# One wide product for the four window sums of a message tile, its diagonal blocks kept and folded

## The chip, the core and the metric

The kernel runs on one NeuronCore of a Trainium2 chip. The metric is the device time in microseconds (us) of one execution. The core has a matrix engine (PE, with its weight loads shown apart as PEld), a vector engine (DVE), a scalar engine (ACT), GpSimd (POOL), which here issues the gathers, and SyncE (SP), which issues the other DMAs. Each engine works through its own instructions in order, and they signal each other by semaphores.

## The reference

The reference is two graph layers on 12500 nodes of 96 features, with 412500 edges sorted by their target node. What matters here is the first layer's message step:

```python
edge_feat = _mlp(edge_attr, W_edge, b_edge, g_edge, beta_edge)
message = jnp.concatenate([x[row], x[col], edge_feat], axis=1)
message = _mlp(message, W_msg, b_msg, g_msg, beta_msg)      # relu(h @ W + b), then a norm over all edges
agg = jax.ops.segment_sum(message, col, num_segments=n)     # sum of the messages of each target node
```

The norm's mean and variance are taken over all edges, so the kernel sums, for each target node, the raw relu outputs and a column of ones, and beside it the squares of all messages; the norm is applied afterwards to the sums.

## The kernel before, in words

Edges are cut into 806 super tiles of 512 edges, four tiles (SUP = 4) of 128 edges each. As edges are sorted by target, the targets of one super tile lie in a window of W = 32 consecutive nodes that begins at `base`. "Tile" below means such a super tile. The program runs through four stretches: a node stage, a first pass over the edges for the statistics of the edge features (in which every sixth tile's gathered rows are also fetched and spilled to memory), the message stage (about 935 to 4340 us), and then the second layer.

The message stage is the one that is changed. It is written out in full, 806 times, on each engine. `msgs.run(engine, step, lag)` calls `step` for k = 0, 1, 2, ... and a step treats tile k in some functions and an earlier one, `msgs.earlier(i, k, n)`, in others. There is no planner: the order of each engine is the order of the calls in its step, and `Signal` objects say what waits for what. For one tile:

- ACT copies the 4 index columns (`copy_indices`, L923), and POOL then gathers 4 x 128 rows of `a_tab` with four indirect DMAs (`gather`, L932), into one of four buffers. The tile that follows in every sixth place is not gathered: SP loads what was spilled (`load_spilled`). A buffer is free when DVE has added its rows (m_pre of tile k-4).
- SP loads the edge features, the target numbers and the window's rows of `b_tab`.
- PE forms the edge product (`edge_product`, L983, bf16, 512 columns); ACT takes its relu into `lhs` (`edge_relu`, L990). DVE writes the transposed one-hots into the lowest 32 rows of `lhs` (`onehot_T`, L998), the window's rows into `rhs` (`window_rows`, L975) and the one-hots `oh` (`onehot`, L1005: 128 edges by 4 x 32).
- PE forms four message products in fp32 (`message_product`, L1017), DVE adds the gathered rows (`add_gathered`, L1030), ACT takes the relu into `msg` (`message_relu`, L1038; 96 columns, and a 97th of ones) and the square (`square`, L1045), which DVE sums up (`accumulate`, L1052).
- PE sums the messages by target (`sum_edges`, L1061): four fp32 products, weights `msg` of 128 x 97, moving `oh` of 128 x 32, that accumulate in one 97 x 32 block of PSUM. DVE adds this block to 32 columns of the node sums `sT` (`add_window`, L1071).

The order of one step k: PE edge_product(k), message_product(k-1), sum_edges(k-2). ACT copy_indices(k), edge_relu(k-2), message_relu(k-3), square(k-3). DVE onehot_T(k), window_rows(k), onehot(k), add_gathered(k-1), accumulate(k-2), add_window(k-2). POOL only gathers, tile after tile. An fp32 product shows in the profile as two records on PE and two on PEld.

Of the kernel before, what the change touches and what calls it, by code (L numbers as in the profile page):

```python
# [17 lines left out]
ALU = mybir.AluOpType  # L18
ACT = mybir.ActivationFunctionType
AX = mybir.AxisListType.X  # L20
# [3 lines left out]
C = 96  # L24
# [4 lines left out]
SUP = 4  # L29
ES = TILE * SUP  # L30
W = P - C
# [64 lines left out]
def gnn_kernel(nc, d, a, out):  # L96
# [4 lines left out]
    with ctx:  # L101
# [7 lines left out]
        def sem(name):  # L109
            stage_sems.append(nc.alloc_semaphore(name))  # L110
            return stage_sems[-1]

        def signal(name, ahead):
            return Signal(sem(name), ahead)
# [33 lines left out]
        ident = sb("ident", [P, P])  # L148
# [39 lines left out]
        msg = sb("msg", [P, 2, SUP, C + 1])  # L188
        sq = sb("sq", [P, 2, SUP, C])
        acc = sb("acc", [P, SUP, C])  # L190
        oh = sb("oh", [P, 4, SUP, W])
        psum = ctx.enter_context(nc.psum_tensor("psum", [P, 8 * 512], FP32))
        bank = [psum[:, i * 512:(i + 1) * 512] for i in range(8)]


        x_flat = x_all[:, :, :].rearrange("p t c -> p (t c)")
# [682 lines left out]
        MT = 2 * SPILL  # L879
        msgs = Turns(SV, MT)  # L880
# [5 lines left out]
        r_mm = signal("r_mm", 4)  # L886
        r_ok = signal("r_ok", 2)
        ohT_ok = signal("ohT_ok", 4)
        oh_ok = signal("oh_ok", 0)
        m_mm = signal("m_mm", 2)  # L890
# [2 lines left out]
        m_sq = signal("m_sq", 2)  # L893
        m_acc = signal("m_acc", 2)
        s_mm = signal("s_mm", 4)
        s_add = signal("s_add", 2)
        def was_spilled(k):
            return k % SPILL == SPILL - 1

# [14 lines left out]
            return bank[2 + k % 2][:, 0:SUP * C].rearrange("p (t c) -> p t c", t=SUP)  # L914

        def ps_s(k):
            return bank[4 + k % 2][0:C + 1, 0:W]

        def copy_indices(act, i, k):
            if msgs.absent(i, k) or was_spilled(k):  # L920
# [131 lines left out]
            dve.tensor_tensor(acc[:, :, :], acc[:, :, :], sq[:, k % 2, :, :], ALU.add).then_inc(m_acc.sem, 1)  # L1052

        def sum_edges(pe, i, k):
            if msgs.absent(i, k):
                return
            pe.wait_ge(m_ok.sem, m_ok.at(MT * i + k))
            pe.wait_ge(oh_ok.sem, oh_ok.at(MT * i + k))
            pe.wait_ge(s_add.sem, s_add.at(MT * i + k - 2))
            for t in range(SUP):  # L1060
                ins = pe.matmul(ps_s(k), msg[:, k % 2, t, :], oh[:, k % 4, t, :], start=(t == 0), stop=(t == SUP - 1))  # L1061
            ins.then_inc(s_mm.sem, 1)

        def add_window(dve, i, k):
            if msgs.absent(i, k):
                return
            base = dve.value_load(base_i[:, bass.ds(MT * i + k, 1)], min_val=0, max_val=N - 1)
            dve.wait_ge(s_mm.sem, s_mm.at(MT * i + k))
            dve.wait_ge(s_add.sem, s_add.at(MT * i + k - 1))
            cols = sT[0:C + 1, bass.ds(base, W)]  # L1070
            dve.tensor_tensor(cols, cols, ps_s(k), ALU.add).then_inc(s_add.sem, 1)  # L1071

        y = gbuf[:, :, :, :].rearrange("p k t c -> p (k t c)")
# [162 lines left out]
        with nc.If(windowed):  # L1242
            with nc.Block() as block:
                @block.gpsimd
                def _(g):
                    def step(i, k):
                        gather(g, i, k)
                    msgs.run(g, step, 0)

                @block.sync  # L1250
                def _(sp):
                    def step(i, k):
                        load_pair(sp, i, k)
                        load_window(sp, i, k)
                        load_spilled(sp, i, k)
                    msgs.run(sp, step, 0)

                @block.tensor
                def _(pe):
                    for x in (r_mm, m_mm, s_mm):  # L1260
                        x.start(pe)
                    def step(i, k):
                        edge_product(pe, i, k)
                        message_product(pe, *msgs.earlier(i, k, 1))
                        sum_edges(pe, *msgs.earlier(i, k, 2))
                    msgs.run(pe, step, 2)

                @block.scalar
                def _(act):
                    for x in (r_ok, m_ok, m_sq):  # L1270
                        x.start(act)
                    def step(i, k):
                        copy_indices(act, i, k)
                        edge_relu(act, *msgs.earlier(i, k, 2))
                        message_relu(act, *msgs.earlier(i, k, 3))
                        square(act, *msgs.earlier(i, k, 3))
                    msgs.run(act, step, 3)

                @block.vector
                def _(dve):  # L1280
                    dve.memset(sT[:, 0:NP], 0.0).then_inc(m0, 1)
                    dve.memset(acc[:, :, :], 0.0).then_inc(m0, 1)
                    dve.wait_ge(m0, 2)
                    for x in (ohT_ok, w_ok, m_pre, m_acc, s_add):
                        x.start(dve)
                    def step(i, k):
                        onehot_T(dve, i, k)
                        window_rows(dve, i, k)
                        onehot(dve, i, k)
                        add_gathered(dve, *msgs.earlier(i, k, 1))  # L1290
                        accumulate(dve, *msgs.earlier(i, k, 2))
                        add_window(dve, *msgs.earlier(i, k, 2))
                    msgs.run(dve, step, 2)
        with nc.Else():
            general_pass("_m", True)

# [700 lines left out]
```

## Time and profile before

| what | value |
|---|---|
| median of the runs | 6518.5 us (6517.94, 6518.5, 6523.41) |
| the profiled execution | 6520.64 us |
| its span, first to last instruction | 6518.9 us |
| PE busy over the span | 5654.6 us (87%) |
| PEld busy | 4382.9 us (67%) |
| DVE busy | 4173.9 us (64%) |
| ACT busy | 3822.2 us (59%) |
| POOL busy | 3237.0 us (50%) |
| mean granted clock of PE | 0.650 |

A row of a group has the line, the engine and the operation, then the written and read tiles with their shapes (partitions x elements, type) and the count, and behind the bar the busy time in us, the mean of one in ns, and the engine's idle time just before these instructions with what ended it. "issue" is idle time in which the engine waited for nothing that the profile shows. In a timeline row the first number is the start in us from the span's start, the second the length. In a windows row the five busy times are those of PE, PEld, DVE, ACT and POOL, in this order, unless the row is of one engine alone. A busy PE is not PE at its peak: matmuls are pipelined and their ends are modelled, so consecutive records overlap.

### The profile page before, as it was taken

To read this page: it belongs to the slowest core of one execution; us is meant where nothing else is said; L and a number is where in the kernel's file an instruction comes from. 1 tells how busy PE (TensorE), PEld (TensorE's weight loads), DVE (VectorE), ACT (ScalarE), POOL (GpSimd) and SP (SyncE) were. 2 spreads that over 40 slices of the span, in tenths; PEclk is the share of its full clock that TensorE was granted. 3 is DMA by queue.
4 is the path that set the end of the run, shared out by engine and by line. 5 is a ranking of instruction groups with operands and counts; after the bars stand their busy time and mean duration, and the time that the engine had idled before them with its cause. 6 is when DMAs were issued, how large, how long until landed. Compare 5 with 4: busy or idle time off the path is not lost. (4 is left out here: it accounts for less than half of the span.)

```text
span 6518.9 us, 128731 instructions
## 1 busy us (share of the span) xinstructions
PE 5654.6 (87%) x38038; PEld 4382.9 (67%) x38038; DVE 4173.9 (64%) x13072; ACT 3822.2 (59%) x7170; POOL 3237.0 (50%) x3406
## 2 busy tenths in 40 slices
PE   6755559999999999999999999977799999999998
PEld 5311127777777777777777777765477777777777
DVE  5577764545454544445454444553799999999996
ACT  3566644434444444444444444433699999999996
POOL 3577757777777777777777777753000000000000
PEclk8555555555555555555555555555799999999998
DMA  4444433333333333333333333321000000000001
GB/s 155 137 123 124 124 83 74 74 76 75 76 75 76 74 76 74 74 76 75 75 75 76 74 75 75 74 79 30 18 2 2 2 2 2 2 2 2 2 2 62
DMA packets 297570, 400.07 MB, mean 61 GB/s; under 512 B 146679, under 2 KB 203015, under 8 KB 296247
## 3 DMA queue, kind: packets, MB, share of 16 engines
q1 hardware_dynamic: 193543, 233.00, 12.1%
q0 software_dynamic: 103344, 158.83, 11.5%
q8 instruction: 323, 5.29, 0.3%
q14 instruction: 360, 2.95, 0.1%
HBM read 333.74 MB, written 57.67 MB: 60 GB/s over the span
## 5 line engine op out<-in xcount | busy, mean ns | idle before, releaser
L932 POOL DMA_INDIRECT gbuf<-a_tab,idxb x2688 | 2580.4, 960 | 859.0 <-issue 812.3
L1718 ACT ACTIVATE nf<-psum 128x600 bf16<-128x600 f32 x3234 | 1824.2, 819 | 4.8 <-PE psum L1709 4.8
L1017 PEld LDWEIGHTS psum<-rhs,lhs 128*128 128x128 f32 x6448 | 1434.3, 327 | 365.8 <-issue 365.8
L1017 PE MATMUL psum<-rhs,lhs 128*128 128x96 f32 x6448 | 1628.7, 434 | 13.5 <-DVE rhs L975 13.5
L1038 ACT ACTIVATE msg<-pre 128x384 f32<-128x384 f32 x806 | 421.8, 523 | 1991.2 <-DVE pre L1030 1988.7
L1030 DVE TENSOR_TENSOR pre<-psum,gbuf 128x384 f32<-128x384 f32 x806 | 448.2, 556 | 1613.6 <-issue 1130.0
L1709 PE MATMUL psum<-x_all 128*128 128x300 bf16 x6468 | 1358.8, 291 | 121.6 <-DVE x_all L1702 44.6
L1061 PE MATMUL psum<-oh,msg 128*97 128x32 f32 x6448 | 1171.1, 344 | 282.4 <-ACT msg L1038 276.7
L1061 PEld LDWEIGHTS psum<-oh,msg 128*97 128x97 f32 x6448 | 1134.0, 282 | 364.1 <-ACT msg L1038 358.7
L1701 DVE TENSOR_SCALAR x_all<-x_all,dstrel 128x600 bf16<-128x600 f16 x3234 | 1193.8, 369 | 87.4 <-PE psum L1709 63.0
L1731 PE MATMUL psum<-x_all,nf 128*128 128x96 bf16 x15400 | 1074.4, 205 | 1.0 <-ACT nf L1718 1.0
L1731 PEld LDWEIGHTS psum<-x_all,nf 128*128 128x128 bf16 x15400 | 937.7, 97 | 165.9 <-issue 1.8
L1702 DVE TENSOR_SCALAR x_all<-x_all,src_i 128x128 bf16<-128x128 bf16 x3234 | 788.2, 244 | 0.0
L1709 PEld LDWEIGHTS psum<-x_all 128*128 128x128 bf16 x6468 | 421.5, 96 | 360.8 <-DVE x_all L1702 241.8
L793 PE MATMUL psum<-x_all,w 36*96 36x512 bf16 x806 | 394.4, 638 | 280.7 <-DMA x_all<-attr_parts 278.1
L836 DVE BATCH_NORM_STATS2 sT<-x_all 96x6 f32<-96x512 f32 x806 | 493.1, 676 | 181.0 <-ACT x_all L813 180.5
L744 POOL DMA_INDIRECT gbuf<-a_tab,idxb x536 | 506.0, 944 | 179.3 <-issue 150.6
L813 ACT ACTIVATE x_all<-psum,par 96x1024 f32<-96x1024 f32 x403 | 425.5, 1105 | 231.7 <-PE psum L793 229.1
L990 ACT ACTIVATE lhs<-psum,par 96x512 f32<-96x512 f32 x806 | 539.2, 669 | 3.9
L983 PE MATMUL psum<-x_all,w 36*96 36x512 bf16 x806 | 530.9, 659 | 4.5 <-DMA x_all<-attr_parts 4.4
L793 PEld LDWEIGHTS psum<-x_all,w 36*96 36x96 bf16 x806 | 118.0, 180 | 556.5 <-DMA x_all<-attr_parts 490.3
L1052 DVE TENSOR_TENSOR acc<-acc,sq 128x384 f32<-128x384 f32 x806 | 441.9, 548 | 0.6 <-ACT sq L1045 0.6
(198 smaller groups left out, 3340.3 us busy)
## 6 DMA issues: line engine op xcount, KB each, us to landing
gbuf<-a_tab,idxb POOLq DMA_INDIRECT x3224
x_all<-dst_row SPq DMA_DIRECT2D x403, 128.0 KB
x_all<-attr_parts SPq DMA_DIRECT2D x807, 36.0 KB
x_all<-attr_parts SPq DMA_DIRECT2D x1209, 24.0 KB
spilled<-gbuf SPq DMA_DIRECT2D x134, 192.0 KB, 1.9
gbuf<-spilled SPq DMA_DIRECT2D x134, 192.0 KB
x_all<-b_tab SPq DMA_DIRECT2D x806, 12.0 KB
attr_parts<-sT SPq DMA_DIRECT2D x72, 136.0 KB, 1.9
```

Source lines behind the costliest of these rows:

```text
L744: g.indirect_dma_start(gbuf[:, j, t, :], None, a_tab[:, :], bass.IndirectOffsetOnAxis(ap=idxb[:, j, t:t + 1], axis=0)).then_inc(x_land[j], 16)
L793: pe.matmul(bank[k % 6][0:C, :], w36[:, :], ek[:, q % NB, k % HG, :], start=True, stop=True).then_inc(e_mm.sem, 1)
L932: g.indirect_dma_start(gbuf[:, k % 4, t, :], None, a_tab[:, :], bass.IndirectOffsetOnAxis(ap=idxb[:, k % 4, t:t + 1], axis=0)).then_inc(g_ ...
L983: pe.matmul(ps_r(k), w36[:, :], rk[:, (k // HP) % 2, k % HP, :], start=True, stop=True).then_inc(r_mm.sem, 1)
L990: act.activation(lhs[0:C, k % 2, :], ps_r(k), ACT.Relu, bias=par[:, B_EDGE:B_EDGE + 1]).then_inc(r_ok.sem, 1)
L1017: ins = pe.matmul(ps_m(k)[:, t, :], lhs[:, k % 2, t * TILE:(t + 1) * TILE], rhs[:, k % 2, :], start=True, stop=True)
L1061: ins = pe.matmul(ps_s(k), msg[:, k % 2, t, :], oh[:, k % 4, t, :], start=(t == 0), stop=(t == SUP - 1))
L1701: dve.tensor_scalar(o_key[:, n % 3, :], iota_k, key_f[:, n:n + 1], None, ALU.is_equal)
L1702: dve.tensor_scalar(o_lo[:, n % 3, :], iota_l, lo_f[:, n:n + 1], None, ALU.is_equal).then_inc(e_oh, 1)
L1709: ins = pe.matmul(ps_a(n)[:, b, :], o_lo[:, n % 3, :], o_key[:, n % 3, b * HB:(b + 1) * HB], start=True, stop=True)
L1718: act.activation(adj[:, g % 2, :, j * SLOT:(j + 1) * SLOT].rearrange("p (b h) s -> p b h s", b=2), ps_a(n).rearrange("p b (h s) -> p b h s ...
L1731: ins = pe.matmul(ps_b(g), adj[:, g % 2, h, :], t3[:, h, :], start=(h == 0), stop=(h == HI - 1))
```

## The change

The four window sums of a tile become one fp32 product. Its weights are all four one-hots side by side (128 edges x 128 columns), its moving operand all four message tiles side by side (128 edges x 4 x 97 = 388 columns). Of the 128 x 388 result only the four diagonal blocks of 32 x 97 are wanted (one-hots of tile t with messages of tile t). ACT copies these four from PSUM into a buffer `diag` of 128 partitions x 97 (`keep_blocks`). A second product (`fold_blocks`), weights `diag` (128 x 97), moving `sel` (128 x 32, four identity matrices of 32 stacked), adds the four blocks and gives the same 97 x 32 block as before, in another bank. DVE adds that to `sT`.

`sel` is made once from the identity by a reduction on DVE, and PE waits for it at the start of the stage. The new order of a step k: PE edge_product(k), message_product(k-1), sum_edges(k-2), fold_blocks(k-4). ACT as before, then keep_blocks(k-4). DVE as before, but add_window(k-5) in place of add_window(k-2). `d_ok`, `f_mm` and the two buffers of `diag` and of the folded block tie these together.

```diff
--- before.py
+++ after.py
@@ -893,7 +893,13 @@
         m_sq = signal("m_sq", 2)
         m_acc = signal("m_acc", 2)
         s_mm = signal("s_mm", 4)
+        d_ok = signal("d_ok", 2)
+        f_mm = signal("f_mm", 2)
         s_add = signal("s_add", 2)
+        sel_ok = sem("sel_ok")
+        X0 = 6 * ES + 2 * C
+        sel = x_flat[:, X0:X0 + W]
+        diag = x_flat[:, X0 + W:X0 + W + 2 * (C + 1)].rearrange("p (b c) -> p b c", b=2)
         def was_spilled(k):
             return k % SPILL == SPILL - 1
 
@@ -914,7 +920,10 @@
             return bank[2 + k % 2][:, 0:SUP * C].rearrange("p (t c) -> p t c", t=SUP)
 
         def ps_s(k):
-            return bank[4 + k % 2][0:C + 1, 0:W]
+            return bank[4 + k % 2][:, 0:SUP * (C + 1)]
+
+        def ps_f(k):
+            return bank[6 + k % 2][0:C + 1, 0:W]
 
         def copy_indices(act, i, k):
             if msgs.absent(i, k) or was_spilled(k):
@@ -1052,28 +1061,42 @@
             dve.tensor_tensor(acc[:, :, :], acc[:, :, :], sq[:, k % 2, :, :], ALU.add).then_inc(m_acc.sem, 1)
 
         def sum_edges(pe, i, k):
+
             if msgs.absent(i, k):
                 return
             pe.wait_ge(m_ok.sem, m_ok.at(MT * i + k))
             pe.wait_ge(oh_ok.sem, oh_ok.at(MT * i + k))
+            pe.wait_ge(d_ok.sem, d_ok.at(MT * i + k - 2))
+            pe.matmul(ps_s(k), oh[:, k % 4, :, :].rearrange("p t w -> p (t w)"),
+                      msg[:, k % 2, :, :].rearrange("p t c -> p (t c)"), start=True, stop=True).then_inc(s_mm.sem, 1)
+
+        def keep_blocks(act, i, k):
+
+            if msgs.absent(i, k):
+                return
+            act.wait_ge(s_mm.sem, s_mm.at(MT * i + k))
+            act.wait_ge(f_mm.sem, f_mm.at(MT * i + k - 2))
+            for t in range(SUP):
+                ins = act.activation(diag[t * W:(t + 1) * W, k % 2, :],
+                                     ps_s(k)[t * W:(t + 1) * W, t * (C + 1):(t + 1) * (C + 1)], ACT.Copy)
+            ins.then_inc(d_ok.sem, 1)
+
+        def fold_blocks(pe, i, k):
+
+            if msgs.absent(i, k):
+                return
+            pe.wait_ge(d_ok.sem, d_ok.at(MT * i + k))
             pe.wait_ge(s_add.sem, s_add.at(MT * i + k - 2))
-            for t in range(SUP):
-                ins = pe.matmul(ps_s(k), msg[:, k % 2, t, :], oh[:, k % 4, t, :], start=(t == 0), stop=(t == SUP - 1))
-            ins.then_inc(s_mm.sem, 1)
+            pe.matmul(ps_f(k), diag[:, k % 2, :], sel, start=True, stop=True).then_inc(f_mm.sem, 1)
 
         def add_window(dve, i, k):
             if msgs.absent(i, k):
                 return
             base = dve.value_load(base_i[:, bass.ds(MT * i + k, 1)], min_val=0, max_val=N - 1)
-            dve.wait_ge(s_mm.sem, s_mm.at(MT * i + k))
+            dve.wait_ge(f_mm.sem, f_mm.at(MT * i + k))
             dve.wait_ge(s_add.sem, s_add.at(MT * i + k - 1))
             cols = sT[0:C + 1, bass.ds(base, W)]
-            dve.tensor_tensor(cols, cols, ps_s(k), ALU.add).then_inc(s_add.sem, 1)
-
-
-
-
-
+            dve.tensor_tensor(cols, cols, ps_f(k), ALU.add).then_inc(s_add.sem, 1)
 
 
         y = gbuf[:, :, :, :].rearrange("p k t c -> p (k t c)")
@@ -1257,29 +1280,34 @@
 
                 @block.tensor
                 def _(pe):
-                    for x in (r_mm, m_mm, s_mm):
+                    for x in (r_mm, m_mm, s_mm, f_mm):
                         x.start(pe)
+                    pe.wait_ge(sel_ok, 1)
+
                     def step(i, k):
                         edge_product(pe, i, k)
                         message_product(pe, *msgs.earlier(i, k, 1))
                         sum_edges(pe, *msgs.earlier(i, k, 2))
-                    msgs.run(pe, step, 2)
+                        fold_blocks(pe, *msgs.earlier(i, k, 4))
+                    msgs.run(pe, step, 4)
 
                 @block.scalar
                 def _(act):
-                    for x in (r_ok, m_ok, m_sq):
+                    for x in (r_ok, m_ok, m_sq, d_ok):
                         x.start(act)
                     def step(i, k):
                         copy_indices(act, i, k)
                         edge_relu(act, *msgs.earlier(i, k, 2))
                         message_relu(act, *msgs.earlier(i, k, 3))
                         square(act, *msgs.earlier(i, k, 3))
-                    msgs.run(act, step, 3)
+                        keep_blocks(act, *msgs.earlier(i, k, 4))
+                    msgs.run(act, step, 4)
 
                 @block.vector
                 def _(dve):
                     dve.memset(sT[:, 0:NP], 0.0).then_inc(m0, 1)
                     dve.memset(acc[:, :, :], 0.0).then_inc(m0, 1)
+                    dve.tensor_reduce(sel, ident[:, :].rearrange("p (t w) -> p w t", w=W), AX, ALU.add).then_inc(sel_ok, 1)
                     dve.wait_ge(m0, 2)
                     for x in (ohT_ok, w_ok, m_pre, m_acc, s_add):
                         x.start(dve)
@@ -1289,8 +1317,8 @@
                         onehot(dve, i, k)
                         add_gathered(dve, *msgs.earlier(i, k, 1))
                         accumulate(dve, *msgs.earlier(i, k, 2))
-                        add_window(dve, *msgs.earlier(i, k, 2))
-                    msgs.run(dve, step, 2)
+                        add_window(dve, *msgs.earlier(i, k, 5))
+                    msgs.run(dve, step, 5)
         with nc.Else():
             general_pass("_m", True)
```

## Rows read from the trace of the kernel before

**Rows 1.** Windows view: span, busy us (count) by engine, clock, DMA share, GB/s

```profile
935.00:4343.00 3408.00, 3119.88 (x13700) 2635.78 (x13701) 1689.52 (x4836) 1383.05 (x3087) 2580.38 (x2688) 0.50 0.31 75
```

**Rows 2.** Waits view of 945 to 4330 us: us in total, times, longest

```profile
DVE pre L1030 <- issue: 1130.0, 424, 5.3
POOL gbuf L932 <- issue: 809.5, 2656, 0.3
DVE pre L1030 <- PE psum L1017: 474.9, 245, 5.2
```

**Rows 3.** Page, costliest groups: busy us, mean ns, idle before and its releaser

```profile
L932 POOL DMA_INDIRECT gbuf<-a_tab,idxb x2688 | 2580.4, 960 | 859.0 <-issue 812.3
...
L1061 PE MATMUL psum<-oh,msg 128*97 128x32 f32 x6448 | 1171.1, 344 | 282.4 <-ACT msg L1038 276.7
```

**Rows 4.** Timeline of POOL: start us, length us, then what

```profile
2621.27 1.17 POOL L932 DMA_INDIRECT gbuf<-a_tab,idxb  x1 [0.30 <-issue]
...
2629.03 0.94 POOL L932 DMA_INDIRECT gbuf<-a_tab,idxb  x1 [0.30 <-issue]
...
2646.68 1.17 POOL L932 DMA_INDIRECT gbuf<-a_tab,idxb  x1 [0.30 <-issue]
```

**Rows 5.** Timeline of PE, a stretch without waits

```profile
2608.19 2.02 PE L1017 MATMUL psum<-rhs,lhs 128*128 128x96 f32 x8
2610.01 1.41 PE L1061 MATMUL psum<-oh,msg 128*97 128x32 f32 x8
2611.34 0.66 PE L983 MATMUL psum<-x_all,w 36*96 36x512 bf16 x1
2611.93 2.02 PE L1017 MATMUL psum<-rhs,lhs 128*128 128x96 f32 x8
```

**Rows 6.** Groups by form, whole span, nearest shapes on PE, ACT and DVE

```profile
L1493 PE MATMUL psum<-gbuf,wc 97*33 97x512 f32 x26 | 24.9, 1061 | 0.0
...
L344 PE MATMUL psum<-dstrel,ones 1*128 1x462 f32 x14 | 11.1, 984 | 7.5 <-DVE flag_f L381 7.5
...
L1483 ACT ACTIVATE gbuf<-psum 97x512 f32<-97x512 f32 x13 | 7.7, 596 | 26.4 <-PE psum L1474 26.4
...
L1616 ACT ACTIVATE wc<-psum 96x32 f32<-96x32 f32 x1 | 0.2, 193 | 2.9 <-PE psum L1600 2.9
...
L1739 DVE TENSOR_REDUCE pre<-psum 128x32 f32<-128x96 f32 x154 | 38.5, 250 | 4.6 <-PE psum L1731 4.6
```

**Rows 7.** Page, costliest groups, weight loads

```profile
L1017 PEld LDWEIGHTS psum<-rhs,lhs 128*128 128x128 f32 x6448 | 1434.3, 327 | 365.8 <-issue 365.8
...
L1061 PEld LDWEIGHTS psum<-oh,msg 128*97 128x97 f32 x6448 | 1134.0, 282 | 364.1 <-ACT msg L1038 358.7
```

**Rows 8.** Windows view of L932 alone, gathers up to 2629 us: busy us (count)

```profile
935.00:2629.00 1694.00, 1285.39 (x1340) 0.50 0.31 75
```

**Rows 9.** Timeline of ACT

```profile
2606.14 0.52 ACT L1045 ACTIVATE sq<-msg 128x384 f32<-128x384 f32 x1
...
2606.67 0.67 ACT L990 ACTIVATE lhs<-psum,par 96x512 f32<-96x512 f32 x1
...
2622.18 0.19 ACT L923 ACTIVATE idxb<-src_i 128x4 int32<-128x4 int32 x1
```

**Rows 10.** Timeline of DVE

```profile
2611.55 0.19 DVE L1071 TENSOR_TENSOR sT<-sT,psum 97x32 f32 x1 [0.27 <-PE psum L1061]
2611.77 0.71 DVE L998 TENSOR_SCALAR lhs<-x_all,winid 32x512 f32<-32x512 int32 x1
...
2621.75 0.49 DVE L998 TENSOR_SCALAR lhs<-x_all,winid 32x512 f32<-32x512 int32 x1
```

**Rows 11.** Timeline, the stage's first gather

```profile
935.19 0.94 POOL L932 DMA_INDIRECT gbuf<-a_tab,idxb  x1 [40.05 <-ACT idxb L923]
```

**Rows 12.** Timeline, the last tile's sum on PE and addition on DVE

```profile
4338.39 1.51 PE L1061 MATMUL psum<-oh,msg 128*97 128x32 f32 x8 [2.81 <-ACT msg L1038]
...
4340.04 0.19 DVE L1071 TENSOR_TENSOR sT<-sT,psum 97x32 f32 x1 [0.56 <-PE psum L1061]
```

## Prediction

> **What bounds the kernel now.** The change touches only the message stage, so I first read the windows view from the stage's first gather to its end [rows 1]: 3408 us of the span of 6518.9, at a granted clock of 0.50, which is the 1.2 GHz level. PE is busy for 3120 us of it (92%), POOL for 2580 (76%), ACT for 1383. By those shares PE looks like the bound. The waits view says otherwise [rows 2]: POOL, 2656 times out of its 2688 gathers in the stage, waited only 0.3 us and for nothing that the profile shows ("issue"), 809.5 us in all. The grouped row gives 960 ns of work for one gather [rows 3]. A gather then comes every 0.960 + 0.305 = 1.265 us. Five tiles in six gather four times (the sixth was spilled and comes back on SP's queue): 20 x 1.265 / 6 = 4.22 us a tile, and 806 tiles make 3399 us. That is the stage. The timeline of POOL shows the cycle: two long gathers at the same place of the pattern, 2621.27 and 2646.68, are 25.41 us apart, with 20 gathers between them [rows 4]. So POOL's issuing of gathers is the bound and never pauses.
>
> PE has room. In a stretch where it waits for nobody, one message product starts at 2608.19 and the next at 2611.93: 3.74 us a tile, in the parts 1.82 (message product), 1.33 (L1061, 2610.01 to 2611.34) and 0.59 (edge product) [rows 5]. That leaves 4.22 - 3.74 = 0.48 us a tile. DVE waits 475 us for PE's L1017 in its L1030, and 1130 us for gathered rows [rows 2]: one tile in six is late by PE, and it is the tile behind the spilled one, whose rows are not urgent.
>
> **The change, part by part.**
> (a) Removed from PE: four products of 97 weight columns and 32 moving columns. L1061 is busy 1171.1 us over 806 tiles, 1.45 us a tile, 0.363 for one product [rows 3].
> (b) Added to PE: one fp32 product with 128 weight columns and 4 x 97 = 388 moving ones. The trace has no such shape. Seven products of 128 by 462 columns (two records each) take 11.1 us, 1.586 each, 3.43 ns a column (L344) [rows 6]: 388 columns are 1.33 us. The isolated ones of 512 columns take 24.9 / 13 = 1.92 us, 3.74 ns a column with their tail (L1493) [rows 6]: 1.45. I take 1.33, since the neighbours keep PE fed.
> (c) Added to PE: the fold, 97 weight columns and 32 moving ones, which is the shape of L1061: 0.363 us.
> Sum on PE: 1.33 + 0.36 - 1.45 = +0.24 us, 3.98 a tile against 4.22. From below: if the wide product hides a weight load of the fold, half of the 0.363, it is +0.06. From above: the slower rate, and one weight load unhidden before each new product (0.327 and 0.282 [rows 7]): 1.45 + 0.36 + 0.33 + 0.28 - 1.45 = 0.97, which would be 4.71; even with one of the two exposed it is 4.38 to 4.43. The nearest row for (b) is the back-to-back one, which has two loads of 128 columns within its 1.586, so I hold to +0.24.
> The Trainium skill, "TensorE: Matmul & The Clock Gate", Part 3 (The mechanism), speaks against that: a weight load overlaps a running matmul only when it goes to another group of rows, and here every one uses all 128 rows. Rows 5 and 7 disagree: eight loads of mean 0.282 add to 2.26 us, and the eight pairs of L1061 pass in 1.41. By that rule both loads of each new product would stand in the open, and the sum would be that of the rival "serial loads" below.
> (d) Added to ACT: four copies PSUM to SBUF of 32 partitions by 97. Two rows enclose them, 96x32 at 193 ns and 97x512 at 596 ns [rows 6]: 0.84 ns a column, so 0.248 each, 0.99 a tile (bounds 0.77 and 2.38). ACT goes from 1383 / 806 = 1.72 to 2.71 us a tile, at worst 4.10, below 4.22. They are queued ahead of the index copy (for which POOL waits), the edge relu (for which PE waits) and the message relu. Their own wait, for the wide product of a tile, is over before ACT gets there: that product is issued two steps of PE earlier, and ACT does a relu and a square (0.52 each) first.
>  - Index copy: the one at 2622.18 belongs to the tile behind the spilled one; its first gather is the one at 2629.03 (1340 gathers lie before it, which is 335 tiles of four [rows 8]). It is 6.7 us early [rows 4, 9]; 1 us off that costs nothing.
>  - Edge relu: in the busiest step the square begins at 2606.14 and the edge relu at 2606.67 [rows 9]. With 1 us between them it ends at 2608.4, when PE wants it at 2608.19 + 0.24 [rows 5]. So one tile in six is later by up to 0.3 us more. It frees the gather buffer of a tile whose gathers start at 2629.03 - 4 x 1.265 = 2624: nobody waits.
> (e) DVE's add_window goes three tiles later, with a wait that is long over. It loses the wait for PE of 0.27 at 2611.55 [rows 10]. The work is the same 806 additions. The one-hot buffer is still four deep and freed by the same signal as before. PE's new waits (for the diagonal copies of two tiles before, for the window sums of two before) end, by the order of the steps, ahead of the message relu that it waits for anyway.
> (f) Ends. At the start DVE reduces 128x128 to 128x32 once; 128x32 from 128x96 takes 0.25 us [rows 6], and the semaphores that let ACT copy the first indices stand behind it: POOL's first gather, at 935.19 after an idle time ended by ACT [rows 11], comes 0.3 us later. At the end the last tile's chain was sum at 4338.39, addition at 4340.04: 1.65 us [rows 12]. Now wide product 1.33 + 0.17 tail, copies 0.99, fold 0.36 + 0.17, handshakes 0.1: 3.1 to 3.3. Plus 1.6.
> Sum of the whole: +1.6 + 0.3 = +1.9 us, call it +2. The profiled execution took 6520.6 us (span 6518.9), the runs shown 6518.5 by their median; so 6522.6 against that execution, and 6520.5 for the median. Where did (a) to (c) go? Into PE's idle time.
>
> **What could still move POOL.** A gather takes 0.94 us in most rows and 0.960 by the mean: 0.020 x 2688 = 54 us are lost in the long ones. They meet L998 on DVE: the gather of 1.17 us began at 2621.27 and L998 at 2621.75, 0.48 into it [rows 4, 10]; at 2611.77 it was L998 itself that took 0.71. Both hold the same resource. L998 follows add_window directly, so (e) shifts it for the one tile in six that waited: 0.27 us earlier by the lost wait, about 0.3 later by (b) to (d). If that one now meets a gather as the one at 2621.27 did, 134 x 0.23 = +31 us; if it met one and now misses, it gives back a share of the 54. Nearest to nought, since the two shifts cancel; I take 0.
>
> **The rivals.**
>  - PE becomes the bound (the other side). It decides once (b) and (c) cost over 1.45 + 0.48 = 1.93 us a tile. With 1.45 + 0.363 and one load of 0.327 in the open they cost 2.14: step 3.74 + 0.69 = 4.43, (4.43 - 4.22) x 806 = +169 us, 6690. For it: PE is already busy 92%, and no row has a 388-column product between narrow ones. Against it: rows 5 and 6 show loads hidden. Chance 0.07.
>  - Serial loads, the same mechanism at its full price: 1.33 + 2 x 0.327 + 0.363 = 2.35 us, step 4.64, +0.42 x 806 = +338 us, 6859. This is the Trainium skill's rule of Part 3 above. Chance 0.03.
>  - L998 meets more gathers: 6551. Chance 0.12.
>  - L998 meets fewer: a third of the 54 us returned, 6502. Chance 0.13.
>  - The wide product, with many more columns a tile, lifts the granted clock from 0.50: PE's step would halve, POOL would still issue every 1.265 us, and only the end would shorten by about 1.5 us: 6519. Chance 0.05.
>  - The forecast: 6520.5, its own range 6508 to 6532. Chance 0.60.
> What a measurement of this kernel can tell from no change is about 0.2%, 13 us. Faster by more: 0.13 (L998 fewer). Slower by more: 0.12 + 0.07 + 0.03 = 0.22. Within: 0.65. The range for 8 in 10 runs from 6500 (all but the best of the fewer-meetings case) to 6560 (over the more-meetings case), and leaves out PE as the bound.
>
> **What the changed profile would show.** PE's step in a stretch without waits 3.9 to 4.1 us; the wide product 1.3 to 1.5 and the fold near 0.36; four ACT copies of about 0.25; POOL's idle time still 0.30 before each gather and its mean near 960 ns; L1071 without a wait for PE; a stage of 3410 us. The prediction is wrong if POOL's idle time is ended by DVE's L1030 or ACT's index copy (PE or ACT had become late), or if the mean gather moves by over 5 ns (13 us).

## The result, and the profile after

The changed kernel takes 6537.2 us (median of 18 runs, 6531.2 to 6542.2) against 6522.3 for the kernel before (18 runs, 6517.9 to 6526.0) beside it. The ratio is 1.0022, with a 95% interval of 1.0015 to 1.0029: about 15 us slower, where +2 was forecast, and a little over the 0.2% (13 us) that the prediction took for no change. It lies inside the predicted range (6500 to 6560), 17 us above the predicted 6520.5 and outside the likeliest case's own range of 6508 to 6532. The profiled execution has a span of 6535.7 us against 6518.9, 16.8 more.

The page's groups of the changed kernel (line, engine, operation, tiles, count | busy us, mean ns | idle before):

```profile
L941 POOL DMA_INDIRECT gbuf<-a_tab,idxb x2688 | 2595.4, 966 | 859.1 <-issue 774.5
...
L1026 PE MATMUL psum<-rhs,lhs 128*128 128x96 f32 x6448 | 1403.5, 387 | 129.0 <-ACT lhs L999 125.5
...
L1070 PE MATMUL psum<-msg,oh 128*128 128x388 f32 x1612 | 1146.5, 809 | 313.9 <-DVE sT L1099 278.0
...
L1080 ACT ACTIVATE x_all<-psum 32x97 f32<-32x97 f32 x3224 | 775.1, 240 | 28.8 <-issue 0.2
```

Against [rows 3], the 2688 gathers are busy 2595.4 us where they were 2580.4, a mean of 966 ns for 960. Their idle time is what it was, 859.1 for 859.0. So 15.0 of the 16.8 us are gathers that took longer, and none is POOL waiting more. The rest stands at the two ends. At the start, with the reduction that makes `sel`:

```profile
934.15 0.24 DVE L1310 TENSOR_REDUCE x_all<-ident 128x32 f32<-128x128 f32 x1
...
935.54 0.94 POOL L941 DMA_INDIRECT gbuf<-a_tab,idxb  x1 [40.42 <-ACT idxb L932]
```

The first gather comes at 935.54, before at 935.19 [rows 11]: +0.35. At the end:

```profile
4348.69 0.95 POOL L941 DMA_INDIRECT gbuf<-a_tab,idxb  x1 [0.30 <-issue]
...
4353.44 0.92 PE L1070 MATMUL psum<-msg,oh 128*128 128x388 f32 x2 [3.62 <-DVE sT L1099]
...
4355.61 0.19 DVE L1099 TENSOR_TENSOR sT<-sT,psum 97x32 f32 x1 [0.64 <-DVE sT L1099]
...
4356.44 0.19 DVE L1099 TENSOR_TENSOR sT<-sT,psum 97x32 f32 x1 [0.64 <-DVE sT L1099]
4357.26 0.19 DVE L1099 TENSOR_TENSOR sT<-sT,psum 97x32 f32 x1 [0.63 <-DVE sT L1099]
```

The last gather ends at 4349.64 and the last window sum begins at 4357.26, 7.62 us later. Before, the last gather ended at 4334.57 and the last window sum began at 4340.04 [rows 12], 5.47 us: +2.15. Sum: 15.0 + 0.35 + 2.15 = 17.5, less 0.3 us of idle time inside the stage and 0.4 behind it.

PE and ACT in the stage. Windows of the whole stage, of a stretch of 18 us and of one of 6 us (us, then busy and count of PE, PEld, DVE, ACT and POOL, granted clock, DMA share, GB/s):

```profile
935.00:4343.00 3408.00, 2967.14 (x10443) 2078.49 (x10442) 1664.56 (x4819) 2199.61 (x6286) 2590.28 (x2683) 0.62 0.32 75
2603.00:2621.00 18.00, 17.48 (x55) 12.30 (x55) 10.42 (x30) 12.79 (x38) 13.73 (x15) 0.50 0.30 71
2624.00:2630.00 6.00, 3.85 (x25) 2.82 (x24) 2.51 (x9) 3.04 (x9) 4.48 (x6) 0.98 0.41 109
```

The granted clock was 0.50 over the stage before [rows 1] and is 0.62 now: it rises to 1.00 and falls back, as the timeline of PE shows, where the same message product takes 2.02 us at 2603.22 and 1.13 at 2624.48.

```profile
2603.22 2.02 PE L1026 MATMUL psum<-rhs,lhs 128*128 128x96 f32 x8
2605.03 1.55 PE L1070 MATMUL psum<-msg,oh 128*128 128x388 f32 x2
2606.38 0.42 PE L1090 MATMUL psum<-x_all 128*97 128x32 f32 x2
2606.73 0.66 PE L992 MATMUL psum<-x_all,w 36*96 36x512 bf16 x1
2607.32 2.02 PE L1026 MATMUL psum<-rhs,lhs 128*128 128x96 f32 x8
...
2611.55 2.02 PE L1026 MATMUL psum<-rhs,lhs 128*128 128x96 f32 x8
...
2624.48 1.13 PE L1026 MATMUL psum<-rhs,lhs 128*128 128x96 f32 x8
...
2626.68 1.13 PE L1026 MATMUL psum<-rhs,lhs 128*128 128x96 f32 x8
```

At the lower level a step is 2607.32 - 2603.22 = 4.10 us (wide product 1.35, fold 0.35), and the next one, 2611.55 - 2607.32, is 4.23; at the higher level a step is 2.20. The three-quarters of the stage at 1.2 GHz did not make PE the bound, and the quarter at 2.4 GHz did not make the kernel faster.

ACT, the step of a tile:

```profile
2604.42 0.52 ACT L1054 ACTIVATE sq<-msg 128x384 f32<-128x384 f32 x1
2604.85 0.99 ACT L1080 ACTIVATE x_all<-psum 32x97 f32<-32x97 f32 x4
...
2606.09 0.68 ACT L999 ACTIVATE lhs<-psum,par 96x512 f32<-96x512 f32 x1
```

The square began at 2604.42 and the edge relu at 2606.09, 1.67 us apart, against 0.53 before [rows 9].

The waits of the stage (us in total, times, longest):

```profile
DVE pre L1039 <- issue: 878.5, 310, 5.0
DVE pre L1039 <- PE psum L1026: 787.7, 356, 5.0
POOL gbuf L941 <- issue: 768.1, 2521, 0.3
...
PEld psum L1026 <- ACT lhs L999: 279.3, 394, 1.3
...
POOL gbuf L941 <- DVE pre L1039: 22.5, 74, 0.3
POOL gbuf L941 <- ACT idxb L932: 21.6, 71, 0.3
...
DVE sT L1099 <- PE psum L1090: 0.3, 1, 0.3
```

DVE's wait for PE before L1039 rose from 475 [rows 2] to 788 us, while its wait there under the name "issue" fell from 1130 to 878.5. PE now waits for ACT's edge relu (L999), 394 times in 806 tiles, so not only for the one tile in six behind a spilled one. DVE's window sum hardly waits for PE any more (once); before, it did so 130 times:

```profile
DVE sT L1071 <- PE psum L1061: 35.8, 130, 0.6
```

POOL's waits for DVE and ACT have a longest of 0.3 us, the same 0.3 that stands before every gather: another name on the same gap.

Which gathers are long? POOL, then DVE:

```profile
2603.87 1.24 POOL L941 DMA_INDIRECT gbuf<-a_tab,idxb  x1 [0.30 <-issue]
...
2607.92 0.94 POOL L941 DMA_INDIRECT gbuf<-a_tab,idxb  x1 [0.30 <-issue]
...
2619.20 1.18 POOL L941 DMA_INDIRECT gbuf<-a_tab,idxb  x1 [0.30 <-DVE pre L1039]
```

```profile
2603.75 0.55 DVE L1061 TENSOR_TENSOR acc<-acc,sq 128x384 f32<-128x384 f32 x1
...
2604.43 0.48 DVE L1007 TENSOR_SCALAR lhs<-x_all,winid 32x512 f32<-32x512 int32 x1
...
2608.46 0.56 DVE L1061 TENSOR_TENSOR acc<-acc,sq 128x384 f32<-128x384 f32 x1
...
2619.01 0.55 DVE L1061 TENSOR_TENSOR acc<-acc,sq 128x384 f32<-128x384 f32 x1
...
2619.70 0.48 DVE L1007 TENSOR_SCALAR lhs<-x_all,winid 32x512 f32<-32x512 int32 x1
```

The prediction blamed DVE's transposed one-hots (now L1007), and they do begin 0.56 us into the gather of 2603.87 and 0.50 into that of 2619.20. But the kernel before has the same start without the loss. Its L998 begins 0.48 us into the gather of 2621.27, which takes 1.17 us [rows 4, 10], and also 0.48 us into that of 2611.29, which takes 0.94:

```profile
2611.29 0.94 POOL L932 DMA_INDIRECT gbuf<-a_tab,idxb  x1 [0.30 <-issue]
```

```profile
2610.73 0.55 DVE L1052 TENSOR_TENSOR acc<-acc,sq 128x384 f32<-128x384 f32 x1
...
2621.07 0.55 DVE L1052 TENSOR_TENSOR acc<-acc,sq 128x384 f32<-128x384 f32 x1
```

What differs is what DVE was doing when the gather began. The accumulation of the squares (L1052, now L1061) ended at 2611.28, just before the short gather, but ran until 2621.62, 0.35 us into the long one. The long gather then ends 0.82 us after it (2622.44). It is the same in the changed kernel: the accumulations end at 2604.30 and 2619.56, the gathers at 2605.11 and 2620.38, 0.81 and 0.82 us later. The accumulation at 2608.46 began inside its gather, and that one takes 0.94.

Counted over all 2688 gathers of a trace, this holds. Of the gathers over 0.96 us, 319 of 342 in the kernel before and 326 of 337 in the changed one end 0.80 to 0.83 us after a DVE instruction that was running as they began (an accumulation, transposed one-hots or window rows). Where the accumulation began over 0.05 us ahead of a gather and ended over 0.15 us into it, the gather was long in 203 of 203 cases before and in 210 of 210 after. For the addition of the gathered rows (L1030, L1039), of the same shape but with one input in PSUM, it was 0 of 155 and 0 of 131. For the transposed one-hots it was 68 of 106 and 41 of 127. So the 15.0 us are the accumulation's: the time above 0.943 us a gather that stands with it rose from 30.7 to 46.4 us, while that of the transposed one-hots fell from 9.9 to 6.0.

### The profile page after: what moved, and what is told of

Same layout as the page of the kernel before. It is cut to its first block and busy times, and to the rows that moved or that the text cites. A ratio compares the mean times of both kernels' runs of the same rounds, so it can differ in the third digit from the quotient of the medians.

```text
span 6535.7 us, 127122 instructions
## 1 busy us (share of the span) xinstructions
PE 5508.3 (84%) x34814; PEld 3834.6 (59%) x34814; DVE 4154.4 (64%) x13073; ACT 4646.9 (71%) x10394; POOL 3252.2 (50%) x3406
## 5 line engine op out<-in xcount | busy, mean ns | idle before, releaser
L941 POOL DMA_INDIRECT gbuf<-a_tab,idxb x2688 | 2595.4, 966 | 859.1 <-issue 774.5
L1039 DVE TENSOR_TENSOR pre<-psum,gbuf 128x384 f32<-128x384 f32 x806 | 448.0, 556 | 1683.8 <-issue 890.0
L1026 PE MATMUL psum<-rhs,lhs 128*128 128x96 f32 x6448 | 1403.5, 387 | 129.0 <-ACT lhs L999 125.5
L1026 PEld LDWEIGHTS psum<-rhs,lhs 128*128 128x128 f32 x6448 | 1228.2, 284 | 438.9 <-ACT lhs L999 282.1
L1070 PE MATMUL psum<-msg,oh 128*128 128x388 f32 x1612 | 1146.5, 809 | 313.9 <-DVE sT L1099 278.0
L1080 ACT ACTIVATE x_all<-psum 32x97 f32<-32x97 f32 x3224 | 775.1, 240 | 28.8 <-issue 0.2
L1090 PEld LDWEIGHTS psum<-x_all 128*97 128x97 f32 x1612 | 417.1, 259 | 469.7 <-issue 433.7
L793 PE MATMUL psum<-x_all,w 36*96 36x512 bf16 x806 | 390.9, 638 | 284.6 <-DMA x_all<-attr_parts 279.9
L1070 PEld LDWEIGHTS psum<-msg,oh 128*128 128x128 f32 x1612 | 378.4, 289 | 379.6 <-ACT msg L1047 376.9
L999 ACT ACTIVATE lhs<-psum,par 96x512 f32<-96x512 f32 x806 | 550.7, 683 | 20.5 <-PE psum L992 0.2
L992 PE MATMUL psum<-x_all,w 36*96 36x512 bf16 x806 | 467.1, 580 | 17.2 <-DVE x_all L1310 15.6
```

Source lines behind the costliest of these rows:

```text
L941: g.indirect_dma_start(gbuf[:, k % 4, t, :], None, a_tab[:, :], bass.IndirectOffsetOnAxis(ap=idxb[:, k % 4, t:t + 1], axis=0)).then_inc(g_ ...
L999: act.activation(lhs[0:C, k % 2, :], ps_r(k), ACT.Relu, bias=par[:, B_EDGE:B_EDGE + 1]).then_inc(r_ok.sem, 1)
L1026: ins = pe.matmul(ps_m(k)[:, t, :], lhs[:, k % 2, t * TILE:(t + 1) * TILE], rhs[:, k % 2, :], start=True, stop=True)
L1070: pe.matmul(ps_s(k), oh[:, k % 4, :, :].rearrange("p t w -> p (t w)"), msg[:, k % 2, :, :].rearrange("p t c -> p (t c)"), start=True, stop ...
L1080: ins = act.activation(diag[t * W:(t + 1) * W, k % 2, :], ps_s(k)[t * W:(t + 1) * W, t * (C + 1):(t + 1) * (C + 1)], ACT.Copy)
```

## Experiments

Each run was timed in five rounds against the kernel before on the same chip. I write loss for the busy time of the 2688 gathers above 2688 x 0.943 = 2534.8 us: 45.6 us in the kernel before, 60.6 in the changed one. T is the theory that POOL's issuing is the whole bound, so that only this loss moves the time, and that it comes from DVE's transposed one-hots. The count above contradicts its second half; the expectations below rest on it. e1 to e4 ran on one chip; e5 to e8, then e9 and e10, then e11 and e12 ran on three others.

**e1 and e2: the same one-hots by a tensor_tensor, in both kernels.**

```diff
-            dve.tensor_scalar(lhs[C:P, ...], dstbc[C:P, ...], winid[C:P, ...], None, ALU.is_equal)
+            dve.tensor_tensor(lhs[C:P, ...], dstbc[C:P, ...], winid[C:P, ...].to_broadcast([W, ES]), ALU.is_equal)
```

> The kernel before, with one edit: the transposed one-hots on DVE (line 998, 32x512) are made by a tensor_tensor compare with winid broadcast, where a tensor_scalar did it. Same output, same place in the order. Theory (T): what lengthens a gather from 0.94 us is that tensor_scalar, when it starts inside a gather, since both want one SBUF port; a tensor_tensor does not take it. Then the mean gather falls from 0.960 to about 0.944 us, the 2688 gathers give back about 43 us, and the time is about 6480 (6470 to 6490), though the compare itself takes longer than 0.486 us (up to 0.7). Rival (R, lateness): the long gathers come from something else in the step (SP's issues, ACT's index copy, landing rows); then the mean stays at 0.960 and the time stays at 6522 within 5.

> The changed kernel with the same edit (tensor_tensor in place of tensor_scalar for the transposed one-hots). T: the 15 us by which the changed kernel is slower are gathers that met the tensor_scalar oftener; without it both kernels have a mean gather of 0.944 us, and this one is only some 2 us above the edited kernel before (start 0.35, end 1.6): about 6482. R (PE or ACT come late for POOL by the longer step): it stays about 15 us above the edited kernel before, 6495 or more, with its gathers' idle time over 0.305 us.

Measured: 6605.7 us for e1 and 6610.8 for e2, against 6521.2 for the kernel before (ratios 1.0126, interval 1.0111 to 1.0142, and 1.0136, 1.0120 to 1.0151). The gathers of e1, those of e2, and the instruction itself in e1 (ns min/median/max):

```profile
L932 POOL DMA_INDIRECT gbuf<-a_tab,idxb x2688 | 2668.4, 993 | 859.6 <-issue 811.7
```

```profile
L941 POOL DMA_INDIRECT gbuf<-a_tab,idxb x2688 | 2668.1, 993 | 859.0 <-issue 764.2
```

```profile
L998 DVE TENSOR_TENSOR lhs<-x_all,winid x806: 686/689/770, 937.4 to 4418.3; 32x512 f32<-32x512 int32 x162
```

The forecast of both theories failed: the edit made gathers longer. The compare takes 0.689 us for 0.486, and the loss went from 46 to 134 us. So my reason, that only a tensor_scalar takes what a gather needs, is wrong. In e1 the compare ran across the start of a gather, as counted above, 199 times, and all 199 were long; 88.0 of the 134 us stand with it. What the pair of runs shows is that one DVE instruction, exchanged for another kind that is 0.2 us longer, moved the time by 84 us while the idle time before the gathers stayed (859.6, 859.0). And the two kernels lie 5 us apart, not 15: with the same loss in both, little is left of the change's cost, as T expected of e2 (2 us) and R did not (15 us).

**e3 and e4: DVE's order turned, in both kernels.**

```diff
-                        onehot_T(dve, i, k)
                         window_rows(dve, i, k)
                         onehot(dve, i, k)
+                        onehot_T(dve, i, k)
```

> The kernel before, with DVE's order in a step turned: window_rows, onehot, then onehot_T (it was first). Same work; the tensor_scalar starts about 0.55 us later. T: its six places in the pattern of 20 gathers fall elsewhere in a gather: the two that cost most now (0.5 to 0.6 us into a gather, 68 to 128 ns each) move to 1.1, where it costs nothing, and the ones at about 0 move to 0.5. The time changes by up to 25 us either way, more likely down, and it does so through the mean gather alone: 2688 x (mean - 0.960) gives the difference within 4 us. R: the order of three DVE instructions that nobody waits for changes nothing, under 4 us.

> The changed kernel with the same turned order on DVE. T: its loss sits at two places of the pattern (gather 7 of 20 with 145 ns, gather 15 with 175 ns above 0.943); both go, others appear: the time moves by 10 to 40 us, more likely down, and again by 2688 x (mean gather - 0.966). R: nothing over 4 us.

Measured: 6540.3 us for e3 (1.0029, 1.0017 to 1.0042) and 6537.6 for e4 (1.0026, 1.0016 to 1.0035; its ten runs from 6527.5 to 6541.7, the profiled one near the low end). Their gathers:

```profile
L932 POOL DMA_INDIRECT gbuf<-a_tab,idxb x2688 | 2597.1, 966 | 859.6 <-issue 814.1
```

```profile
L941 POOL DMA_INDIRECT gbuf<-a_tab,idxb x2688 | 2585.5, 962 | 859.0 <-issue 757.9
```

The channel (the gathers' own length) came as T said, and in e3 the size, but not the direction. The order of instructions that nobody waits for costs the kernel before 19 us; 16.7 of them are gathers (2597.1 - 2580.4). In e4's profiled run the gathers fell by 9.9 us against the changed kernel, and the span by 9.9 (6535.7 - 6525.8); its median did not fall, so runs of one kernel seem to differ in this loss too (only one run of each was profiled). The span less the gathers' busy time is the same in all six kernels that ran where POOL is the bound:

| kernel | span | gathers busy | span less busy |
|---|---|---|---|
| before | 6518.9 | 2580.4 | 3938.5 |
| changed | 6535.7 | 2595.4 | 3940.3 |
| e1 | 6608.6 | 2668.4 | 3940.2 |
| e2 | 6611.2 | 2668.1 | 3943.1 |
| e3 | 6537.5 | 2597.1 | 3940.4 |
| e4 | 6525.8 | 2585.5 | 3940.3 |

That is the strongest evidence for the bound: busy times of 2580 to 2668 us, and 4.6 us between the smallest and the largest rest. e3 also has a long gather with no transposed one-hot in it. The gather of 2622.34 ends at 2623.55, 0.81 us after the accumulation, which ended at 2622.74:

```profile
2622.34 1.21 POOL L932 DMA_INDIRECT gbuf<-a_tab,idxb  x1 [0.30 <-issue]
```

```profile
2622.19 0.55 DVE L1052 TENSOR_TENSOR acc<-acc,sq 128x384 f32<-128x384 f32 x1
```

**e5 to e12: parts of the change alone, and the one-hots off DVE.** These eight kernels ran in three groups, beside which the kernel before itself took 7691, 7762 and 7756 us, so they ran where POOL is not the bound. They are told for what they can say. The edits: one-hots on ACT (e5, e9, e12 in the kernel before, e8 in the changed one),

```diff
-                        onehot_T(dve, i, k)
...
+            act.activation(to, dstbc[...], ACT.Abs, bias=winid[...], scale=-1.0).then_inc(abs_ok.sem, 1)
+            act.wait_ge(abs_ok.sem, abs_ok.at(MT * i + k))
+            act.activation(to, to, ACT.Relu, bias=ones[C:P, 0:1], scale=-1.0).then_inc(ohT_ok.sem, 1)
```

ACT's copies alone (e6; what they copy is not meaningful and is not used),

```diff
+            for t in range(SUP):
+                ins = act.activation(spare[t * W:(t + 1) * W, k % 2, :], bank[6 + k % 2][...], ACT.Copy)
```

and the later add_window alone (e7, e10, e11):

```diff
-            return bank[4 + k % 2][0:C + 1, 0:W]
+            return bank[4 + k % 4][0:C + 1, 0:W]
...
-                        add_window(dve, *msgs.earlier(i, k, 2))
+                        add_window(dve, *msgs.earlier(i, k, 4))
```

> The kernel before, with the transposed one-hots taken off DVE: ACT makes them in two steps, abs(winid - target) and relu(1 - that), beside its edge relu of the same tile; the output is the same. ACT goes from 1.72 to about 3.0 us a tile, under the 4.22 of POOL. Theory (T: time is a constant plus what gathers lose to DVE's instructions, mainly the one of line 998 that this takes away): the mean gather falls from 0.960 to 0.945 to 0.950, and the time by 25 to 42 us, to about 6485. Rival (R: the loss is not that instruction's, any DVE work back to back does it): the mean gather stays at 0.957 or more and the time within 8 us of before.

> The kernel before, with one part of the change alone: ACT makes the four copies of 32x97 from PSUM after its square, of blocks that nobody uses (their content is not meaningful). The four sums on PE, and DVE, are as before. This is the part that makes the edge relu late, and by it the tile behind the spilled one by about 0.3 us. If ACT's copies are what moved the gathers' losses (theory A): the loss at gather 7 of the 20 grows as in the changed kernel, +10 to +15 us. If the lost wait of add_window is (theory W): this alone stays within 5 us of before. In both the gathers' idle time stays 0.305.

> The kernel before, with one part of the change alone: add_window two tiles later (step lag 4 for 2, four PSUM banks for 2), so that DVE never waits for PE there. Theory W: the one-hots of the tile behind the spilled one start 0.27 us earlier, now at 0.3 to 0.5 into a gather, where they cost 70 to 180 ns: +9 to +20 us. Theory A (the copies): this alone is within 5 us of before.

> The changed kernel with the transposed one-hots on ACT as in the other. ACT's sum would be 2.7 + 1.35 = 4.05 us a tile against POOL's 4.20, and copies, relus and one-hots stand in one queue. If ACT keeps up (T), it is 2 to 5 us above the edited kernel before. If ACT's queue becomes the bound (rival), it is slower by more, by what ACT's step is over 4.20: at 4.3 a tile +80 us, and POOL's gathers then wait for DVE's line L1030 or ACT's index copy.

> The kernel of e5 once more (the kernel before, transposed one-hots on ACT in two steps, not on DVE). In the run of e5 the kernel before itself took 7691 us, with stalls of 5 to 15 us on every engine, so POOL's gathers were not the bound there; this asks again where the kernel before takes about 6520. T: the time is a constant of about 6473 us plus what the 2688 gathers lose above 0.943 us, and DVE's instruction of line 998 makes most of that loss: the mean gather 0.945 to 0.955, the time 6480 to 6505. R: mean gather 0.957 or more, time within 8 us of before. If the stalls come back, its gathers' mean alone can be read (e5: 0.955).

> The kernel of e7 once more (the kernel before, add_window two steps later and nothing else of the change), for the same reason. Theory W (the lost wait of add_window puts the transposed one-hots of the tile behind the spilled one at 0.3 to 0.5 us into a gather): +9 to +20 us, and the loss sits at gather 7 of the pattern of 20. Theory A (the loss of the changed kernel comes by ACT's copies, which make the edge relu and by it that tile late): within 5 us of before.

> The kernel of e7 and e10 a third time, in the hope of a chip on which the kernel before takes about 6520 us and POOL never waits. Theory W (the lost wait of add_window moves the transposed one-hots into the gather): +9 to +20 us, all of it in the gathers' busy time. Theory A (ACT's copies and the longer step on PE do it, by making the tile behind the spilled one 0.3 us later): within 5 us of before. If the kernel before takes about 7700 again, rows land about 12 us after their gather was issued, POOL waits for free buffers, and the difference says nothing on this.

> The kernel of e5 and e9 a third time, for the same reason. T: where POOL is the bound, taking the transposed one-hots off DVE brings the mean gather from 0.960 to 0.945 to 0.955 us and the time to 6480 to 6505. R: time within 8 us of before. Where rows land late (kernel before at about 7700), it is slower by 20 to 80 us, as in e5 and e9, since ACT's queue then stands in the loop from landing to the next gather.

Measured, as ratios to the kernel before beside them: one-hots on ACT 1.0026 (1.0015 to 1.0037), 1.0105 (1.0085 to 1.0124), 1.0094 (1.0072 to 1.0116), and in the changed kernel 1.0352 (1.0334 to 1.0371); copies alone 1.0026 (1.0016 to 1.0036); later add_window alone 1.0073 (1.0056 to 1.0090), 1.0078 (1.0059 to 1.0098), 1.0081 (1.0058 to 1.0104). e8 is 249 us above e5, as its rival said in kind: POOL's idle time is ended by ACT's index copy. How those runs differ from the others shows in the window of 1000 to 4000 us of e7, its waits there, and its gathers:

```profile
1000.00:4000.00 3000.00, 2030.76 (x8944) 1709.85 (x8944) 1156.27 (x3218) 958.06 (x2054) 1745.02 (x1794) 0.50 0.25 58
```

```profile
DVE pre L1030 <- remote: 1155.9, 147, 15.6
ACT lhs L990 <- remote: 841.7, 116, 15.0
POOL gbuf L932 <- ACT idxb L923: 705.8, 136, 51.9
```

```profile
L932 POOL DMA_INDIRECT gbuf<-a_tab,idxb x2688 | 2620.6, 975 | 1862.6 <-ACT idxb L923 1061.3
```

The engines are as fast as elsewhere (a gather's median is 0.944 us, the granted clock 0.50), but DVE and ACT wait up to 15.6 us for something that the profile calls remote, and POOL is idle for 1862.6 us, 1061.3 of them ended by ACT's index copy. The 58 GB/s for 75 [rows 1] are no cause by themselves: about the same bytes move in a longer stage. I read the loop through landing, add, relu and index copy as the bound there; no run changed it alone. So these times don't tell which part of the change moved the loss where POOL is the bound; that stays open. In that other regime the later add_window costs 0.8% by itself, three times over, which I can't explain from the rows.

One reading holds in both regimes, since it is of the gathers' own length. One-hots on ACT (e5, e8), and on DVE (e6; e7 above); e9 and e12 have 2565.0 and 2567.8, e10 and e11 have 2628.7 and 2618.5:

```profile
L933 POOL DMA_INDIRECT gbuf<-a_tab,idxb x2688 | 2567.4, 955 | 1864.5 <-issue 874.3
```

```profile
L942 POOL DMA_INDIRECT gbuf<-a_tab,idxb x2688 | 2549.7, 949 | 2137.2 <-ACT idxb L933 1256.7
```

```profile
L933 POOL DMA_INDIRECT gbuf<-a_tab,idxb x2688 | 2651.6, 986 | 1777.8 <-issue 899.0
```

With the one-hots on ACT the loss above 2534.8 us is 15 to 33 us; with them on DVE it is 84 to 117. The mean is 955 ns where e5 expected 945 to 950 and its rival 957 or more, and 954 and 955 in e9 and e12, inside their 945 to 955. But it is not mostly the one-hots' own loss that went. By the instruction that ended 0.80 to 0.83 us before a long gather did, the loss divides so (us):

| kernel | loss | accumulation | transposed one-hots | window rows and `oh` |
|---|---|---|---|---|
| before | 45.6 | 30.7 | 9.9 | 2.7 |
| changed | 60.6 | 46.4 | 6.0 | 4.6 |
| e1 | 133.6 | 30.4 | 88.0 | 14.1 |
| e2 | 133.3 | 36.6 | 76.4 | 18.9 |
| e3 | 62.3 | 51.6 | 3.9 | 3.6 |
| e4 | 50.7 | 36.4 | 2.2 | 9.0 |
| e5 (one-hots on ACT) | 32.6 | 24.8 | none | 7.1 |
| e7 (later add_window) | 85.8 | 71.8 | 11.4 | 0.5 |

In e5 the accumulation runs across fewer starts of gathers than in e7 (95 for 227). The kernel before itself was not profiled on these chips, so what the one-hots alone are worth there is not shown. That taking them off DVE would bring the kernel under 6520 us where POOL is the bound was expected and never seen: three runs of it met the other regime.

## Why the prediction was right or wrong

- **The bound.** Right. POOL's issuing sets the stage; the table of spans shows it to 5 us. PE's share of 92% did not matter.
- **(a) to (c), PE.** A step of 3.98 us was forecast, 4.10 measured at the lower clock: the wide product 1.35 for 1.33, the fold 0.35 for 0.36; what I took off was the busy time of L1061, 1.45, though its part of the step was 1.33 in the very rows cited: busy times of PE have modelled ends that overlap, and a step is summed from starts. Single steps take 4.23, but on the whole it stays under the 4.22 of POOL, which did not wait: the 0.48 us of idle time took it. The Trainium skill's rule in "TensorE: Matmul & The Clock Gate", Part 3 (The mechanism), that a weight load overlaps a matmul only in another group of rows (the same section also lets it go ahead into a background buffer), is not borne out: two records of 388 columns with their loads pass in 1.35 us, and the rival "serial loads" (4.64 us a step) is ruled out.
- **(d), ACT.** The four copies measure 240 ns each for 248. Taken as hidden, and they were for POOL. The edge relu came 1.1 us later behind the square, for 1 us forecast; PE waited for it up to 1.3 us and in about half of the tiles, which I had put at 0.3 us for one tile in six, and DVE's wait for PE rose by 313 us. Neither made POOL wait. They may well have moved DVE's accumulation against the gathers; no run separates that.
- **(e), the loss in long gathers.** This is the step that failed. I had two shifts of L998 of about 0.3 us cancel and took 0; the loss rose by 15.0 us. By the prediction's own sign it was wrong here: the mean gather moved by 15.0 us / 2688 = 5.6 ns, over the 5 ns that it set. The channel (DVE lengthens gathers) was right, the instruction was not. The gathers wait for what DVE is running as they begin, mostly the accumulation (30.7, then 46.4 us), which the prediction never looks at; L998's own share fell by 3.9 us. The trace before could have shown it, with L998 beginning 0.48 us into two gathers, one long and one not. The later add_window did lose its wait for PE, as said (130 times before, once after). What set the accumulation later against the gathers stays open.
- **(f), the ends.** +0.35 for 0.3 and +2.15 for 1.6: the last three window sums come one by one, 0.82 us apart, each behind the one before it, which the chain of the last tile alone did not count.
- **The clock.** I gave a rise 0.05. It rose to 1.00 for a quarter of the stage, and as forecast for that case it bought nothing, since POOL issues at its own pace. By the Trainium skill's "TensorE: Matmul & The Clock Gate", Part 1, sustained activity releases the throttle; here the clock moves up and down in a stage in which PE is busy 87% of the time, and before it stayed at 0.50 with PE busy 92% [rows 1], so the traces agree only in part.
- **The chances.** 6537 lies between the forecast and the rival "L998 meets more gathers". That the range holds it is in part luck: its upper end was set for more loss by L998, and L998 lost less. A loss that changes by 17 us when DVE's order is turned, as in e3, should have had a wider "same" case and more weight above 13 us.

## What to carry to other kernels

Find the engine that never waits, and check the bound by a difference that stays constant (span less its busy time) over several kernels; then a change elsewhere is worth what it does to that engine's own instructions. When that engine's instructions have a long tail, look at what is already running on the others as they begin, measure from its end, and look for one of its instructions that is short though the suspect stands at the same place. An edit that only shifts a partly idle engine can move the time by more than the work it adds. And time a variant on more than one chip before trusting a bound: here it was another one on three of four.

## What the runs showed of the hardware

- A gather of 128 rows takes 0.944 us of POOL in the median. When DVE is in the 128x384 accumulation (both inputs in SBUF) as the gather begins, the gather ends 0.81 to 0.82 us after that instruction does, and up to 1.32 us after its own start in the kernel before. An addition of the same shape with one input in PSUM does not do this (0 of 155). The accumulation begun 0.54 us into a gather left it at 0.94 us.
- It goes the other way too: a 32x512 compare begun 0.48 us into a gather of 0.94 us took 0.71 us itself instead of 0.49 [rows 10]. As a tensor_tensor the compare cost the gathers more, not less (loss 134 us for 46). What the two engines share is not shown by these runs.
- The same kernel took 6521 us on one chip and 7691 to 7762 on three others, with engines equally fast; why is not shown.
- With wide fp32 products PE's granted clock went from 0.50 to a mean of 0.62 in the stage, in stretches of 1.00.
